# A gated attention-and-FFN block on one core: w2 turned by DMA, late scores on GpSimd, the last tile in halves

## The chip, the cores and the metric

The kernel runs on 1 core of one Trainium2 chip. The metric is the time of one execution on the device in microseconds, as the median of the runs.

## The reference

x is 4 x 512 rows of 512 values. First each row gets a term made of a sigmoid of pairwise scores and of its own normalised values; then a gated FFN with quantized weights (ternary) and quantized activations (8 bits) is added.

```python
def xattn(ctx, adj, W, b):                  # ctx: 4 x 512 x 128, adj = layernorm(x): 4 x 512 x 512
    si = einsum('bnd,d->bn', ctx, W[0, :128]);  sj = einsum('bnd,d->bn', ctx, W[0, 128:])
    return 0.6 * sigmoid(si[:, :, None] + sj[:, None, :] + b[0]) + 0.4 * adj
def weight_quant(w):
    scale = 1.0 / clip(mean(abs(w)), 1e-5);  return clip(round(w * scale), -1, 1) / scale
def bitlinear(x, w):                        # w1, w2: 1408 x 512, w3: 512 x 1408
    xn = x * rsqrt(mean(x * x, -1) + 1e-6);  s = 127 / clip(max(abs(xn), -1), 1e-5)
    return einsum('bsd,hd->bsh', clip(round(xn * s), -128, 127) / s, weight_quant(w))
x = x + tanh(g_xattn[0]) * xattn(ctx_512, layernorm(x), W, b)
y = layernorm(x)
x = x + tanh(g_ffn[0]) * bitlinear(silu(bitlinear(y, w1)) * bitlinear(y, w2), w3)
```

## The kernel before

The 2048 rows make 16 tiles of 128 rows, four to a batch. Tile i holds rows 128 i to 128 i + 127, one row to a partition. Everything runs from one program with an order written out by hand for each engine (SP from L322, GpSimd from L541, ScalarE from L763, VectorE from L1078, TensorE from L1354); semaphores tie them together. An engine that waits holds everything behind it in its order.

**Weights.** Each weight is loaded in four pieces (L295). The absolute values are summed by ScalarE (L643) and VectorE (L967), a matmul with ones adds over partitions (L1243), and VectorE makes the scale (`scale_w`, L975). w1 is turned by TensorE from float32, one row block of 128 at a time (`turn_rows`, L1265), and quantized on the way out of PSUM (L658, L1006) with a clip behind it (L1012). w2 is quantized in place, in six groups of two row blocks (`conv_w`, L505 and L992; GpSimd has groups 1 to 4), turned by TensorE (`turn_w`, L1276) and written out by ScalarE with a sign (L653) or by VectorE with a limit (L1001). w3 is quantized by GpSimd, clipped by VectorE (L1021) and turned by DMA (`turn_w3`, L302).

**Scores.** TensorE turns the context of a batch (`turn_ctx`, L1208), makes both scores as products (`scores`, L1218), and spreads them as a row over all partitions (`spread_scores`, L1228); ScalarE copies that row to SBUF (L685) and makes tanh of row plus own score for each tile (`score`, L689), in a ring of four.

**A tile.** `stats_x` (L918) and GpSimd's `slopes_x` (L435) give the layer norm's slope, `intercept` (L927) its offset; an affine and `make_x` (L945) give the new x, `max_x` (L957) and `square_x` its scale, `quant_x` (L488) the quantized tile, which SP turns by DMA (`turn_x`, L306). Tiles go in units (L41): 0; 1; 2 and 3; 4 and 5; and so on in pairs. TensorE makes the gate product into three banks and the up product into three others (`product`, L1294); ScalarE's `silu` (L716) empties the first, VectorE's `hidden` (L1028) the second, so gate product t + 1 waits for silu(t) and up product t + 1 for hidden(t). `max_h` (L1041), `quant_h` (L515) and `turn_h` (L312) prepare the last product (L1323), eleven matmuls of 512 columns; `finish` (L735) and `add_x` (L536, L1050) scale and add, and `store` (L318) writes the tile. The last tile's hidden values are turned by TensorE in two parts (`turn_last`, L1344).

GpSimd's `dequant_up(0)` (L473) is what `hidden(0)` waits for beside the up product, and `hidden_floors` (L429) writes two constants behind each slot of the ring `hid`, which lies where w2 was loaded, so it waits until w2 has been read.

## Time and profile before

| | |
|---|---|
| median of 3 runs | 158.2 us (157.78 to 158.7) |
| span of the profiled execution | 155.3 us |
| TensorE, VectorE busy | 139.7 us, 117.9 us |
| ScalarE, GpSimd busy | 107.3 us, 101.0 us |
| mean granted clock of TensorE | 0.978 |
| DMA | 26.94 MB, of it 13.89 MB read from HBM |

The profile is one execution; the difference of span and median lies before the first and behind the last instruction. In the rows, PE is TensorE, DVE VectorE, ACT ScalarE, POOL GpSimd, SPq the queue of SyncE, which issues the DMAs. L and a number is the line of the kernel. A granted clock of 1.00 is 2.4 GHz and of 0.50 is 1.2 GHz. Rows of a timeline that stand behind each other on an engine overlap by up to 0.1 us, so a step is read from start to start.

### The profile page before, as it was taken

How to read it: one execution, taken by the hardware profiler on the slowest of the kernel's cores; microseconds unless marked ns; L12 is line 12 of the kernel's file. 1: busy time of each engine (PE TensorE's matmuls, PEld its weight loads, DVE VectorE, ACT ScalarE, POOL GpSimd, SP SyncE). 2: the span in 40 equal slices, each digit the busy share in tenths (PEclk: the TensorE clock that was granted, in tenths of full speed). 3: DMA queues.
4: the chain of work that ended last, by engine and by line, in shares of the span. 5: the costliest groups of instructions: out<-in, count | busy, mean ns of one | idle time of the engine just before them, and what ended most of it. 6: DMA issues, size and time to landing. Idle time of an engine off the chain costs nothing.

```text
span 155.3 us, 2445 instructions
## 1 busy us (share of the span) xinstructions
PE 139.7 (90%) x743; PEld 76.7 (49%) x743; DVE 117.9 (76%) x180; ACT 107.3 (69%) x177; POOL 101.0 (65%) x155
## 2 busy tenths in 40 slices
PE   0984965798998999999999999999999999999991
PEld 0883854365555455444444444444454444454540
DVE  0338998998889999999979966489579184669441
ACT  3279998979598489967799286532999636772720
POOL 3302617999892791785989985669968999436210
PEclk9999599779999999999999999999999999999999
DMA  4899999999214189733193695453362807654313
GB/s 146 289 406 395 407 402 414 392 364 347 61 38 93 34 168 212 151 62 69 35 199 64 152 113 146 100 104 126 101 160 60 241 9 189 160 97 93 135 74 129
DMA packets 45237, 26.94 MB, mean 173 GB/s; under 512 B 35751, under 2 KB 37800, under 8 KB 45224
## 3 DMA queue, kind: packets, MB, share of 16 engines
q1 hardware_dynamic: 45216, 26.78, 60.9%
q8 instruction: 6, 0.10, 0.3%
q14 instruction: 7, 0.06, 0.1%
q10 hardware_dynamic: 8, 0.00, 0.0%
HBM read 13.89 MB, written 4.19 MB: 116 GB/s over the span
## 4 chain that ended last, share of the span: by engine, by line
PE 72%; DVE 11%; DMA 5%; POOL 4%; issue 3%; ACT 2%; SPq 1%; DVEq 0%; ACTq 0%; POOLq 0%
PE ps L1307 46%; PE ps L1341 24%; DMA raw_room<-in_L_ffn_w_dram 5%; DVE raw L1038 2%; DVE bn L922 2%; ACT w2T L656 1%; DVE w_abs L972 1%; POOL ln_r L440 1%; DVE w3q L1026 1%; DVE c_all L953 1%; DVE w1T L1009 1%; POOL raw L509 1%; DVE x_top L962 1%; PE ps L1290 1%; POOL slope L443 1%
## 5 line engine op out<-in xcount | busy, mean ns | idle before, releaser
L1307 PE MATMUL ps<-w1T,xqT 128*128 128x512 f16 (+1 forms) x192 | 42.3, 372 | 0.0
L1307 PE MATMUL ps<-w2T,xqT 128*128 128x512 f16 (+1 forms) x192 | 40.7, 361 | 1.1 <-ACT w2T L656 0.6
L1341 PE MATMUL ps<-w3T,hqT 128*128 128x512 f16 x176 | 40.1, 379 | 0.0
L1038 DVE SCALAR_TENSOR_TENSOR raw<-ps,deq,raw_room 128x1408 f32<-128x1408 f32 x16 | 26.9, 1683 | 16.6 <-PE ps L1307 11.2
L721 ACT ACTIVATE raw_room<-ps,deq 128x1408 f32<-128x1408 f32 x16 | 22.9, 1432 | 15.9 <-PE ps L1307 15.8
L521 POOL TENSOR_SCALAR hq<-raw,h_scale 128x1408 f16<-128x1408 f32 x15 | 23.8, 1590 | 9.9 <-DVE h_scale L1048 9.6
L1307 PEld LDWEIGHTS ps<-w1T,xqT 128*128 128x128 f16 x192 | 19.2, 100 | 20.6 <-issue 2.2
L1307 PEld LDWEIGHTS ps<-w2T,xqT 128*128 128x128 f16 x192 | 18.6, 98 | 20.9 <-DVE raw L1038 0.8
L1341 PEld LDWEIGHTS ps<-w3T,hqT 128*128 128x128 f16 x176 | 17.2, 98 | 19.3
L1045 DVE TENSOR_REDUCE h_top<-raw 128x1 f32<-128x1409 f32 x16 | 25.8, 1610 | 0.2
L732 ACT ACTIVATE junk<-raw 128x1410 f16<-128x1410 f32 x16 | 21.9, 1372 | 1.5 <-DVE raw L1038 1.3
L741 ACT ACTIVATE out_ring<-ps,x_mean,h_deq 128x512 f32<-128x512 f32 x14 | 10.8, 773 | 13.4 <-DMA out_dram<-out_ring 8.1
L494 POOL TENSOR_SCALAR xq<-c_all,x_scale 128x512 f16<-128x512 f32 x16 | 11.1, 695 | 10.9 <-DVE x_scale L965 10.6
L922 DVE BATCH_NORM_STATS2 bn<-c_all 128x6 f32<-128x512 f32 x16 | 10.3, 678 | 4.2 <-DMA c_all<-in_x_dram 4.2
L539 POOL TENSOR_TENSOR out_ring<-out_ring,c_all 128x512 f32<-128x512 f32 x9 | 12.4, 1375 | 0.0
L953 DVE SCALAR_TENSOR_TENSOR c_all<-th_ring,t,c_all 128x1024 f32<-128x1024 f32 (+1 forms) x9 | 10.4, 1158 | 0.6 <-ACT c_all L682 0.5
L455 POOL TENSOR_SCALAR c_all<-c_all,slope,icept 128x512 f32<-128x512 f32 x8 | 6.3, 796 | 6.2 <-DVE icept L935 6.2
L708 ACT ACTIVATE junk_x<-c_all 128x514 f16<-128x514 f32 x16 | 10.0, 622 | 0.6 <-DVE c_all L953 0.6
L962 DVE TENSOR_REDUCE x_top<-c_all 128x2 f32<-128x1026 f32 (+1 forms) x9 | 9.8, 1091 | 0.1
L532 POOL TENSOR_TENSOR h_r<-h_sq,minus_half 128x2 f32<-128x2 f32 (+1 forms) x9 | 6.1, 678 | 5.7 <-ACT junk L732 5.7
L651 ACT ACTIVATE junk<-raw 128x1408 f16<-128x1408 f32 (+2 forms) x6 | 8.2, 1358 | 1.4 <-DMA raw<-in_L_ffn_w_dram 1.3
L699 ACT ACTIVATE th_ring<-sj_wide,s_half 128x512 f32<-128x512 f32 x12 | 8.6, 716 | 0.7 <-DVE c_all L953 0.7
(99 smaller groups left out, 173.5 us busy)
## 6 DMA issues: line engine op xcount, KB each, us to landing
c_all<-in_x_dram SPq DMA_DIRECT2D x16, 256.0 KB, 9.5
out_dram<-out_ring SPq DMA_DIRECT2D x16, 256.0 KB, 2.1
raw<-in_L_ffn_w_dram SPq DMA_DIRECT2D x4, 704.0 KB, 11.2
raw_room<-in_L_ffn_w_dram SPq DMA_DIRECT2D x3, 768.0 KB, 8.2
raw<-in_L_ffn_w_dram SPq DMA_DIRECT2D x3, 768.0 KB, 11.7
hq<-in_ctx_dram SPq DMA_DIRECT2D x4, 256.0 KB, 10.2
raw_room<-in_L_ffn_w_dram SPq DMA_DIRECT2D x1, 512.0 KB, 10.3
raw<-in_L_ffn_w_dram SPq DMA_DIRECT2D x1, 512.0 KB, 10.6
```

What stands on the lines that cost most here:

```text
L494: g.tensor_scalar(xq[:, i % XQ, :], c_all[:, i, 0:D], x_scale[:, i:i + 1], QMAX * TINY, ALU.mult, ALU.mult).then_inc(xq_done, 1)
L521: g.tensor_scalar(hq[:, t % HQ, :], hid[:, t % HS, 0:H], h_scale[:, t:t + 1], QMAX * TINY, ALU.mult, ALU.mult).then_inc(hq_done, 1)
L539: g.tensor_tensor(o, o, c_all[:, t, 0:D], ALU.add).then_inc(out_done[t % OUTS], 1)
L721: s.activation(gate[:, t % GATES, :], ps_gate[:, 0:H], ACT.Silu, scale=deq[:, 0, t:t + 1]).then_inc(silu_done, 1)
L732: s.activation(junk[:, t % 2, 0:H + 2], hid[:, t % HS, 0:H + 2], ACT.Square, scale=H_SQUARE, accum_out=h_sq[:, t:t + 1]).then_inc(h_sq_don ...
L922: v.bn_stats(bn[:, i, :], c_all[:, i, 0:D]).then_inc(bn_done, 1)
L953: v.scalar_tensor_tensor(out=c_all[:, lo:hi, 0:D], in0=th_ring[:, lo % 4:lo % 4 + hi - lo, :], scalar=t03[:, 0:1], in1=c_all[:, lo:hi, 0:D ...
L962: v.tensor_reduce(out=x_top[:, lo:hi], in_=c_all[:, lo:hi, 0:D + 1], axis=AX_X, op=ALU.max, apply_absolute_value=True).then_inc(x_topped, 1)
L1038: v.scalar_tensor_tensor(out=hid[:, t % HS, 0:H], in0=ps_up[:, 0:H], scalar=deq[:, 1, t:t + 1], in1=gate[:, t % GATES, :], op0=ALU.mult, o ...
L1045: v.tensor_reduce(out=h_top[:, t:t + 1], in_=hid[:, t % HS, 0:H + 1], axis=AX_X, op=ALU.max, apply_absolute_value=True).then_inc(h_topped, 1)
L1307: last = m.matmul(bank[:, lo:hi], xqT[:, i % XT, k, :], wT[w][:, k, lo:hi], start=(k == 0), stop=(k == KD - 1))
L1341: last = m.matmul(ps_y[t % 2], hqT[:, t % HT, k, :], w3T[:, :, k, :], start=(k == 0), stop=(k == KH - 1))
```

## The change

- **Rows four to a partition.** A tile holds every fourth row of a batch, so a partition holds four neighbouring rows over the four tiles. The pieces of x and of the output stay 2 KB; a context load has one piece of 2 KB in a partition and not four of 512 B. ScalarE therefore reads spread scores from PSUM with a stride.
- **w2.** Quantized into a tile of its own, w2q (in the place of hqT), by VectorE (groups 0 and 5), ScalarE (1) and GpSimd (2 to 4); VectorE clips each group (`clip_w2`); SP turns it by DMA in three chunks of 4, 4 and 3 row blocks (`turn_w2`). TensorE no longer turns it, and nobody writes it out of PSUM. The three parts of up product 0 wait for one chunk each. `hidden_floors` waits for all six clips.
- **Late scores.** For batches 2 and 3 GpSimd multiplies the context by W (`ctx_product`), VectorE sums (`sum_scores`), SP stores the row of scores to DRAM (`store_sj`) and loads it back to all partitions (`spread_sj`).
- **The last tile.** Quantized by VectorE in one instruction, turned by DMA; its product is made in two halves of 256 columns in two banks, and `finish` and `store` work by halves (`finish_half`, `store_half`).
- **Loads.** Tiles 4 and 5 come before w3; W, the context of batch 2 and tiles 6 and 7 behind it, and the turns of w2 stand before tiles 8 to 15. The context of batch 3 comes much later.
- All five engines have new orders.

```diff
--- before.py
+++ after.py
...
-    x_t = x.rearrange("b (t p) d -> (b t) p d", p=P)
-    out_t = out.rearrange("b (t p) d -> (b t) p d", p=P)
-    ctx_t = ctx_in.rearrange("b (t p) d -> b p t d", p=P)
+    x_rows = x.rearrange("b (p t) d -> b t p d", p=P)
+    out_rows = out.rearrange("b (p t) d -> b t p d", p=P)
+    x_t = [x_rows[i // TB, i % TB] for i in range(T)]
+    out_t = [out_rows[i // TB, i % TB] for i in range(T)]
+    ctx_t = ctx_in.rearrange("b (p t) d -> b p t d", p=P)
+    sj_rows = nc.dram_tensor("sj_rows", (B, N), F32, kind="Internal").ap()
...
-    CONV_POOL = [[], [1, 2, 3, 4], [0, 1, 2, 3]]
+    CONV_ACT = [[], [1], []]
+    CONV_POOL = [[], [2, 3, 4], [0, 1, 2, 3]]
...
+    PRODUCTS = 2
+    LATE = [n for n in range(B) if n >= PRODUCTS]
+    HALF = D // 2
+    TURNS = [(0, 2), (2, 4), (4, 6)]
...
-        w2T = sb("w2T", [P, KD, H], F16)
+        w2T = sb("w2T", [P, KH, KD, P], F16)
...
+        w2q = hqT[:, :, :, :].rearrange("p s k c -> p (s k c)").rearrange("p (t d) -> p t d", d=D)
...
+        w_wide = sb("w_wide", [P, 2, DC])
+        ctx_w = hqT[:, 2:4, :, :].rearrange("p s k c -> p (s k c)")[:, 0:4 * TB * DC].bitcast(F32).rearrange(
+            "p (u t d) -> p u t d", t=TB, u=2)
+        s_sums = sb("s_sums", [P, B, 2, TB])
...
+            def store_sj(n):
+
+                sp.wait_ge(scores_sb, n + 1)
+                sp.dma_start(sj_rows[n].rearrange("(p t) -> p t", p=P),
+                             s_half[:, n, 1, :]).then_inc(sj_stored[n - PRODUCTS], 16)
+
+            def spread_sj(n):
+
+                sp.wait_ge(sj_stored[n - PRODUCTS], 16)
+                sp.dma_start(sj_wide[:, n - len(DIRECT), :],
+                             sj_rows[n:n + 1].broadcast_to([P, N])).then_inc(sj_in[n - PRODUCTS], 16)
+
+            def turn_w2(c):
+
+                sp.wait_ge(w2_clip, TURNS[c][1])
+                lo, hi = CHUNKS[c][0] // P, CHUNKS[c][1] // P
+                sp.dma_start_transpose(w2T[:, lo:hi, :, :].rearrange("p t k c -> p (t k) c"),
+                                       w2q[:, lo:hi, :].rearrange("p t d -> p (t d)")).then_inc(w2_in[c], 16)
...
             def turn_h(t):
-                sp.wait_ge(hq_done, t + 1)
+                if t == T - 1:
+                    sp.wait_ge(hq_last, 1)
+                else:
+                    sp.wait_ge(hq_done, t + 1)
+                if t == 0:
+                    for c in range(len(CHUNKS)):
+                        sp.wait_ge(w2_in[c], 16)
+                if t == 2:
+                    sp.wait_ge(s_summed, len(LATE))
...
             def hidden_floors():
 
-                pool.wait_ge(wT_ps, NG)
+                pool.wait_ge(w2_clip, NG)
...
-                    g.tensor_scalar(raw_low[w][:, lo:hi, :], raw[w][:, lo:hi, :], w_scale[:, w:w + 1], 1.0, ALU.mult,
-                                    ALU.mult).then_inc(w_q_pool, 1)
+                    g.tensor_scalar(w2q[:, lo:hi, :], raw[w][:, lo:hi, :], w_scale[:, w:w + 1], TINY, ALU.mult,
+                                    ALU.min).then_inc(w_q_pool, 1)
...
+            def ctx_product(n):
+
+                if n == PRODUCTS:
+                    pool.wait_ge(w_wide_in, 16)
+                    for c in range(len(CHUNKS)):
+                        pool.wait_ge(w2_in[c], 16)
+                else:
+                    pool.wait_ge(s_summed, n - PRODUCTS)
+                pool.wait_ge(ctx_ld[n], 16)
+                g.tensor_tensor(ctx_w[:, :, :, :], ctx_sb[n].rearrange("p (u t) d -> p u t d", u=1).broadcast_to([P, 2, TB, DC]),
+                                w_wide[:, :, :].rearrange("p u (t d) -> p u t d", t=1).broadcast_to([P, 2, TB, DC]),
+                                ALU.mult).then_inc(ctx_times_w, 1)
...
+            def conv_w(w, n):
+                act.wait_ge(w_scaled, w + 1)
+                lo, hi = GROUPS[n]
+                s.activation(w2q[:, lo:hi, :], raw[w][:, lo:hi, :], ACT.Copy, scale=w_scale[:, w:w + 1]).then_inc(w_q_act, 1)
...
+                if n in DIRECT:
+                    act.wait_ge(sj_ps, n + 1)
+                    s.activation(th_ring[:, i % 4, :].rearrange("p (c k) -> p c k", k=TB),
+                                 ps_y[1].rearrange("p (k c) -> p c k", k=TB), ACT.Tanh, bias=s_half[:, n, 0, i % TB:i % TB + 1],
...
+            def sum_scores(n):
+
+                dve.wait_ge(ctx_times_w, n - PRODUCTS + 1)
+                v.tensor_reduce(out=s_sums[:, n, :, :], in_=ctx_w[:, :, :, :], axis=AX_X, op=ALU.add).then_inc(s_summed, 1)
+                dve.wait_ge(s_summed, n - PRODUCTS + 1)
+                v.tensor_scalar(s_half[:, n, :, :], s_sums[:, n, :, :], 0.5, b_quarter[:, 0:1], ALU.mult, ALU.add).then_inc(scores_sb, 1)
...
+            def clip_w2(n):
+                lo, hi = GROUPS[n]
+                if n in CONV_DVE[1]:
+                    dve.wait_ge(w_q_dve, count(CONV_DVE, 1, n))
+                elif n in CONV_ACT[1]:
+                    dve.wait_ge(w_q_act, count(CONV_ACT, 1, n))
+                else:
+                    dve.wait_ge(w_q_pool, count(CONV_POOL, 1, n))
+                v.tensor_scalar(w2q[:, lo:hi, :], w2q[:, lo:hi, :], TINY, -TINY, ALU.min, ALU.max).then_inc(w2_clip, 1)
...
-                            w_left(w, NG - 1)
+                            rows_left([9, 10, 5][c])
+                            pe.wait_ge(w2_in[c], 16)
...
-                if t < T - 1:
-                    pe.wait_ge(hT_in[t % HQ], 16 * (t // HQ + 1))
+                pe.wait_ge(hT_in[t % HQ], 16 * (t // HQ + 1))
+                if t == T - 1:
+                    pe.wait_ge(silu_done, T)
+                    for n in range(2):
+                        for k in range(KH):
+                            last = m.matmul(ps_last[n], hqT[:, t % HT, k, :],
+                                            w3T[:, n * KD // 2:(n + 1) * KD // 2, k, :], start=(k == 0), stop=(k == KH - 1))
+                        last.then_inc(y_ps, 1)
+                    return
...
```

Of the new orders, the stretches that the prediction speaks of. Numbers are the arguments; x, h and w are the tiles, a pair (w, n) a weight and its part.

```
SP:     w3 (4 loads), load_w_wide, load_ctx 2, load_x 6 7, turn_w2 0 1 2, load_x 8 9, turn_x 2, load_x 10 11, turn_x 3,
        turn_w3 0, load_x 12, turn_w3 1, turn_x 4, load_x 13 14, turn_w3 2, turn_x 5, load_x 15, store_sj 2, turn_h 0,
        turn_w3 3, load_ctx 3, turn_x 6, spread_sj 2, turn_h 1, turn_x 7, turn_h 2, store_sj 3, spread_sj 3, turn_h 3,
        turn_h 4, turn_x 8, store 0, turn_h 5, ... turn_h 14, store 9, turn_h 15, store 10 to 14, store_half 0 1
GpSimd: ... quant_x 1, conv_w (1,2), slopes_x 2, conv_w (1,3) (1,4), hidden_floors, affine_x 2 3, dequant_gate 0, step_x 1,
        slopes_x 3, conv_w (2,0), dequant_x 1, dequant_up 0, quant_x 2, conv_w (2,1), step_x 2, quant_x 3, dequant_x 2,
        conv_w (2,2), ctx_product 2, step_x 3, quant_x 4 5, dequant_x 3, quant_h 0, conv_w (2,3), dequant_h 0, step_x 4,
        quant_x 6, quant_h 1 2, mean_x 0, ctx_product 3, slopes_x 4, dequant_x 4, quant_h 3, quant_x 7, affine_x 8 9, ...
VectorE: ... scale_w 1, stats_x 2, weight_factor 0, conv_w (1,0), clip_w2 0, evac_rows 10, clip_w1 2, conv_w (1,5),
        clip_w2 1, sum_w (2,0), intercept 2, clip_w2 2 3, weight_factor 1, clip_w2 4 5, stats_x 3 4, make_x 2, scale_w 2,
        weight_factor 2, max_x 2, intercept 3, hidden 0, clip_w3 0 1, make_x 3, intercept 4, hidden 1, max_h 0, max_x 3,
        hidden 2, max_h 1, sum_scores 2, clip_w3 2, hidden 3, make_x 4, clip_w3 3, max_x 4, hidden 4, max_h 2 3,
        stats_x 5 6, hidden 5, sum_scores 3, intercept 5, max_h 4, intercept 6, make_x 5, hidden 6, max_h 5, max_x 5, ...
ScalarE: ... evac_x 0, evac_rows 8, sum_w (2,0), scores_out 1, evac_rows 9, conv_w (1,1), th_neg_x 0, square_x 1,
        sum_w (2,1), evac_x 1, sum_w (2,2), silu 0, score 4 5 6, square_x 2, affine_x 4, score 7, affine_x 5, silu 1, ...
        silu 15, finish 11 12, square_h 14 15, finish 13
TensorE: ... turn_rows 10, gate 0, turn_x 1, sum_w 2, up 0, gate 1, up 1, ... gate 5, up 5, last 0, gate 6, last 1, up 6,
        gate 7, last 2, up 7, last 3, gate 8, last 4, up 8, ... gate 11, up 11, last 5, last 6, gate 12, last 7, up 12, ...
        last 10, gate 15, up 15, last 11 to 15
```

## Rows read from the trace of the kernel before

**Rows 1.** The page, part 1: busy us, share of the span, instructions of each engine.

```profile
PE 139.7 (90%) x743; PEld 76.7 (49%) x743; DVE 117.9 (76%) x180; ACT 107.3 (69%) x177; POOL 101.0 (65%) x155
```

**Rows 2.** The table of windows, one stretch: busy us of each engine, clock, DMA, GB/s.

```profile
48.49:151.95 103.46, 103.44 (x515) 49.85 (x515) 80.22 (x102) 69.39 (x109) 72.04 (x99) 1.00 0.53 119
```

**Rows 3.** The chain of waits in order of time: start us, us, what.

```profile
60.55 0.44 PE ps L1232 x4
...
125.19 14.26 PE ps L1307 x72
...
146.57 0.61 PE ps L1350 x11
147.19 4.76 PE ps L1341 x22
...
152.07 0.75 DVE out_ring L1075
```

**Rows 4.** The timeline of PE, the first gate and up product: start us, us, what.

```profile
28.91 4.23 PE L1307 MATMUL ps<-w1T,xqT 128*128 128x512 f16 x12
...
36.72 2.54 PE L1307 MATMUL ps<-w2T,xqT 128*128 128x512 f16 x12 [0.61 <-ACT w2T L656]
```

**Rows 5.** The table of windows inside the first gate product.

```profile
30.00:31.00 1.00, 1.00 (x4) 0.34 (x3) 1.00 (x1) 1.00 (x3) 1.00 (x2) 0.50 1.06 369
```

**Rows 6.** The timeline of DVE, w2's scale and the steps of a tile.

```profile
24.98 0.16 DVE L982 RECIPROCAL w_scale<-w_step 128x1 f32<-128x1 f32 x1
...
69.45 1.68 DVE L1038 SCALAR_TENSOR_TENSOR raw<-ps,deq,raw_room 128x1408 f32<-128x1408 f32 x1
71.05 0.45 DVE L935 TENSOR_SCALAR icept<-th_sum,t_neg,slope_mean 128x1 f32<-128x1 f32 x2
71.42 1.61 DVE L1045 TENSOR_REDUCE h_top<-raw 128x1 f32<-128x1409 f32 x1
...
73.17 1.28 DVE L953 SCALAR_TENSOR_TENSOR c_all<-th_ring,t,c_all 128x1024 f32<-128x1024 f32 x1
74.37 1.28 DVE L922 BATCH_NORM_STATS2 bn<-c_all 128x6 f32<-128x512 f32 x2
...
75.78 1.19 DVE L962 TENSOR_REDUCE x_top<-c_all 128x2 f32<-128x1026 f32 x1
...
77.09 1.60 DVE L1045 TENSOR_REDUCE h_top<-raw 128x1 f32<-128x1409 f32 x1
```

**Rows 7.** Line L1026: duration ns min/median/max, first and last start.

```profile
L1026 DVE TENSOR_SCALAR w3q<-w3q x4: 506/1078/1315, 45.1 to 57.5; 128x1408 f16<-128x1408 f16 x4
```

**Rows 8.** The timeline of POOL: conversions, quantizations, and the first and last of slopes.

```profile
26.91 6.33 POOL L509 TENSOR_SCALAR raw<-raw,w_scale 128x1024 f16<-128x1024 f32 x4
...
65.44 0.70 POOL L494 TENSOR_SCALAR xq<-c_all,x_scale 128x512 f16<-128x512 f32 x1
66.11 1.44 POOL L521 TENSOR_SCALAR hq<-raw,h_scale 128x1408 f16<-128x1408 f32 x1
...
67.79 0.25 POOL L439 TENSOR_SCALAR ln_ve<-ln 128x4 f32<-128x4 f32 x1 [0.24 <-DVE ln L925]
...
69.62 0.20 POOL L444 TENSOR_TENSOR slope_mean<-slope,ln 128x4 f32<-128x4 f32 x1
```

**Rows 9.** Line L539: duration ns min/median/max, first and last start.

```profile
L539 POOL TENSOR_TENSOR out_ring<-out_ring,c_all x9: 1262/1274/2181, 77.1 to 131.1; 128x512 f32<-128x512 f32 x9
```

**Rows 10.** The DMA issues by line: what, count, KB, median us to landing.

```profile
hqT<-hq SPq DMA_TRANSPOSE x15, 3.5
xqT<-xq SPq DMA_TRANSPOSE x14, 2.4
...
out_dram<-out_ring SPq DMA_DIRECT2D x16, 256.0 KB, 2.1
```

**Rows 11.** The table of windows while hqT, w3T and xqT are turned together.

```profile
60.00:62.00 2.00, 2.00 (x14) 1.25 (x12) 1.89 (x4) 2.00 (x4) 0.44 (x1) 1.00 1.13 214
```

**Rows 12.** The groups by line: the spread scores read by ACT from PSUM.

```profile
L699 ACT ACTIVATE th_ring<-ps,s_half 128x512 f32<-128x512 f32 x4 | 2.7, 673 | 0.0
```

626 lines of the change are left out of this document (286 added, 340 removed).

## The prediction

> **What bounds the kernel now.** I read the page first: TensorE is busy 139.7 of 155.3 us, VectorE 117.9 [rows 1]. The table of windows then says where TensorE has room: from 48.49 to 151.95 us it is busy 103.44 of 103.46 us at a granted clock of 1.00 [rows 2]. The chain of waits agrees: from there it is TensorE's, with no wait on another engine, until the last `finish` [rows 3]. A product (12 matmuls, or 11 against w3) steps 2.375 us there (six in 14.26 [rows 3]), so 43 products take 102.1 us, and two insertions stand between them: spreading the scores of batch 3 (0.44) and turning the last tile (0.61) [rows 3]. So the end is set by (a) when the unbroken stretch begins and (b) what stands in it besides products. Before it, VectorE, ScalarE, GpSimd and the loads take turns: the first gate product starts at 28.91 and takes 4.2 us [rows 4] because the granted clock is 0.50 (1.2 GHz) in it [rows 5], and the first up product starts at 36.72.
>
> The span is 155.3; the median of the runs is 158.2, so 2.9 us lie outside. I add a change of the span to 158.2. A measurement of this kernel can tell about 0.5% (0.8 us) from no change.
>
> **TensorE's own savings.** Gone from it: 44 transposes of w2, the context transposes, score products and spreads of batches 2 and 3, and the 11 transposes of the last tile. Those before 48.49 us count only if the new start of the unbroken stretch is set by TensorE; I find below that it isn't. In the stretch 0.44 + 0.61 = 1.05 us go. The last product as 22 matmuls of 256 columns moves the same columns: 0. The up products read w2T in pieces of 128 columns now, as the products with w3T do, and those step 2.38 [rows 3]: 0. The last `finish` covers 256 columns, about 0.45 instead of 0.75 us [rows 3]: 0.3 us less.
>
> **When the stretch begins.** I lay the new orders out engine by engine, with steps from start to start in the rows. Up to the scale of w2 little changes: VectorE has it at 25.1 us now [rows 6] and at 25.5 in the new order. Then w2 takes the new way. VectorE: statistics of tiles 2 and 3 to 27.0, conversion and clip of group 0 to 28.1, row block 10 to 28.7. ScalarE reaches row block 9 only at about 29.4, since it first sums the first w3 piece, and the w3 loads come 0.26 MB later, about 0.7 us at 369 GB/s [rows 5]; w1's last clip then ends at 29.9, conversion of group 5 and clip of group 1 at 31.5, the sum of w3's piece at 33.0, an intercept at 33.4, and clips of groups 2 to 5 at 34.9 (0.35 each, 0.51 of [rows 7] cut to 1024 elements). GpSimd's three conversions at 1.4 to 1.6 us [rows 8] end by about 32.
>
> Clips have a range: the four of w3 took 0.51 to 1.32 us for 1408 elements [rows 7]; the six new ones have 1024 or 512. At 0.35 GpSimd stands idle beside the last four; the upper end is 0.9 more for each of the six, 3 us in all if none found it idle. The long ones of w3 ran beside GpSimd's conversions and quantizations. The Trainium skill, "SBUF — State Buffer", section "SBUF: two separate sides", says that a VectorE instruction of this kind and one of GpSimd exclude each other for their whole length; the trace agrees, 0.51 against 1.32. By that rule the last four clips, with GpSimd waiting, stay short.
>
> The DMA turns three chunks of 16, 16 and 12 blocks. A turn of 11 blocks lands 3.5 us after its issue, one of 4 blocks 2.4 [rows 10], and back to back they move 214 GB/s with all 16 engines taken [rows 11]. The last chunk, issued at about 35.5 behind two of 2.5 us each, lands at 39.5 (bounds 38.4, issue plus 3.5, and 41). So the first up product ends at 40.0, against 39.1 now.
>
> Behind the clips comes the dearer part. GpSimd's `hidden_floors` waits for all six clips, with all its work queued behind it: two affines (36.8), the gate factor (37.1), step_x 37.9, the slopes of four tiles (2.0 by [rows 8], 39.95), w3's first conversion (41.4), the up factor (41.9). `hidden(0)` waits for that last one: 41.9 to 43.5. The second gate product runs 40.0 to 42.4, or 44.1 if the clock is at 1.2 GHz as in the first [rows 4, 5], since TensorE has only the chunks of one product between 31 and 40 us. Up product 1 starts at 43.5 to 44.1 and ends 46.2; gate product 2 ends 48.6 (`silu(1)` 45.2 and the turn of tile 2 at 45.0 are in time); `hidden(1)` ends 47.8. So up product 2 starts at **48.6** against 48.49: +0.1. Both the lost clock and most of the saved PE work vanish here. If w2 or GpSimd are 1.5 us quicker or later, this start moves by that.
>
> The Trainium skill, "TensorE: Matmul & The Clock Gate", section "What's actually happening", says that an idle engine falls to 1.2 GHz. The trace agrees that the level falls behind thin work [rows 5].
>
> **Inside the stretch.** TensorE wants, from 48.6 in steps of 2.375: g4 at 55.7, u4 58.1, u5 62.9, L0 65.2, L1 70.0, u6 72.4, g7 74.7, L2, u7, L3, g8 at 84.2 (g gate, u up, L last products). The engines behind it, by [rows 6, 8]: VectorE does `hidden` in 1.60, `max_h` 1.75, `make_x` 1.20, two `stats` 1.41, `max_x` 1.31 (pairs of tiles). The two sums of scores are new: a reduce of 1024 elements and a small one, 1.4 us each, and `ctx_product` (1024 outputs from two inputs) has no like in the trace; the nearest row is GpSimd's addition of two 512-wide tiles, 1.27 [rows 9], so 2.5 for its 1024 outputs, bounds 2.0 (the two fixed starts counted once) and 4.4 (one such addition took 2.18).
> - GpSimd ends w3's third conversion at 49.4, `ctx_product(2)` at 51.9, step_x 52.7, `quant_x(4)` 53.4; turned by 55.8: g4 waits 0.1.
> - VectorE from there: hidden(2) 52.6, max_h(1) 54.3, scores 55.7, clip 56.4, hidden(3) 58.0, make_x 59.2, clip 59.8, max_x 61.1, hidden(4) 62.7 (just in time for u5), max_h(2) 64.4, max_h(3) 66.1, stats of units 5 and 6 at 68.9, hidden(5) 70.5.
> - GpSimd: `quant_h(2)` 65.9, `ctx_product(3)` 68.6, then `slopes_x(4)`, which needs those stats: 70.95; factors 71.15; `quant_h(3)` 72.6; `quant_x(7)` 73.3 (1.44 and 0.70 by [rows 8]); the turn of tile 7 lands at 75.7. g7 wants to start at 74.7: **1.0 us of stall**. Now `quant_x(7)` is done at 66.1 [rows 8], long before its product.
> - SP: `turn_h(2)` (its slot holds ctx_w) waits for the second sum of scores, 71.9, and stands behind turn_x(7): lands 78.2, L2 wants 78.1. Behind it `spread_sj(3)` waits for its store (2.1 us, as an output store [rows 10]), with turn_h(3) (L3) and turn_x(8) (g8) queued: lands 82.9 and 84.5, wanted at 82.8 and 85.2. No cost, no slack.
> - After g8 VectorE is ahead again (hidden(7) 89.5, wanted 90.5).
> - The end: last tile turned by DMA: hidden(15) 1.6, max_h 1.75, quantization 0.9, turn 3.5 [rows 10] = 7.8 us, behind four products (9.5): hidden. `finish(13)` now follows both last squares on ScalarE and a store; 0.2 us in hand, price up to 1.
>
> The other moves cost nothing that I can see. Strided rows of x keep pieces of 2 KB, and those of ctx grow from 512 B to 2 KB; the context's gain of some 0.1 us ends in front of w1's loads. ScalarE now reads the spread scores from PSUM with a stride, five times, 0.6 to 0.7 us each now [rows 12]: bounds 0 and 0.7 more for each, 3 us in all, of which two reads (1.4) precede w1's sum; no row has such a read, I take 0 as the count of elements is the same.
>
> **Sum**: +0.1 (start) - 1.05 (insertions) + 0.1 + 1.0 (g4, g7) - 0.3 (tail) = -0.15 us. Span 155.15, time 158.05, which I round to **158.0**.
>
> **Rivals.**
> 1. *The covers hold* (faster). Up product 2 starts 1 to 2 us sooner (the last turn lands at 38.4, clock stays high) and the stall of g7 is not there because VectorE's chain starts sooner too: -0.15 - 1.0 - 1.5 = -2.65, 155.5. For it: GpSimd and ScalarE are only 65% and 69% busy [rows 1]. Against: three serial waits in front of `hidden(0)`. Range 154.5 to 157.3. Chance 0.31.
> 2. *GpSimd's products are dear* (slower). At 4.4 instead of 2.5 us, quant_x(4) is 1.9 late for g4 and quant_x(7) again for g7 (its slopes then start at 70.5): +1.9 + 1.5 = 3.4, 161.5. It decides from 3.0 us a product on. For it: one addition of 2.18 us; against: the median of nine is 1.27 [rows 9], and its place beside VectorE's one-input reduces. With queue stalls at L2 and L3 of 1 us: 159 to 161. Chance 0.25.
> 3. *The queue of SP is the bound*: turn_h(2) to turn_x(8) late by more than the 0.1 of slack, 0.5 to 2 us, 158.6 to 160. It decides from a `sum_scores(3)` 0.5 us late. Chance 0.06 beside what lies in 2, 0.02 of it still within the bound.
> 4. *The change of w2 is no different way*: the turn hides wholly and the start is as now, no stall: -1.35, 156.85; in 1.
>
> My own case has 0.38 (156.9 to 159.0), 0.06 of it below 157.4, where faster begins. So faster 0.31 + 0.06, same 0.32 + 0.02, slower 0.25 + 0.04. Range for 8 in 10: 154.8 to 161.0; my likeliest case alone 156.9 to 159.0.
>
> **What would show it.** The first up product ending at about 40 with gaps between its three chunks; GpSimd idle some 3 us before `hidden_floors`; `hidden(0)` released by GpSimd; up product 2 at 48 to 49.5; TensorE's idle just before gate product 7 released by a DMA of xqT; two GpSimd products of 2.5 us; the last PE insertion gone. Wrong if TensorE is unbroken from before 47 us, if the products take over 3 us, or if L2 or L3 wait on hqT by over 0.5.

## The result, and the profile after

The changed kernel takes **167.1 us** (median of 4 runs, 166.68 to 167.44) against 158.45 of the kernel before on the same chip (157.78 to 160.47): ratio 1.0593, interval 1.0539 to 1.0646. It is slower by 6%; forecast were 158.0 us and a range that ended at 161.0. Ratios leave out executions more than 1.5% above the fastest of their kernel, and medians count them, which matters for e7, e11 and e15 below (159.06, 160.9 and 161.7 us without them).

The profiled execution took 166.95 us, its span 165.1, so 1.85 us lie outside the span. The 2.9 us that the prediction took for the kernel before are a median less the span of one execution: in the 62 executions of the kernel before that ran beside the experiments 1.7 to 1.9 us lie outside. So its profiled execution, with a span of 155.3, must have been one of the quick ones, at about 157.1 us, an estimate; the spans differ by 9.8 us and the medians by 8.65.

The page, part 1 and the row of TensorE's clock in part 2 (the kernel before: [rows 1]):

```profile
PE 138.3 (84%) x667; PEld 72.3 (44%) x667; DVE 121.2 (73%) x184; ACT 102.0 (62%) x170; POOL 109.3 (66%) x156
...
PEclk9998775985589999999999999999999999999999
```

TensorE's instructions fell from 743 to 667, as the diff says. GpSimd's busy time rose by 8.3 us, though its two new products of the context with W take only 4.7. The clock is low twice, in slices 5 to 7, which end at 28.9 us, and again in slices 10 and 11, 37 to 45 us, where up product 0 runs.

The timeline of TensorE: start us, us, what, and in brackets the idle time before it and what ended it. It answers [rows 4] and, for the end, [rows 3]:

```profile
36.89 1.86 PE L1354 MATMUL ps<-w2T,xqT 128*128 128x512 f16 x4 [2.14 <-DMA w2T<-hqT]
41.28 1.87 PE L1354 MATMUL ps<-w2T,xqT 128*128 128x512 f16 x4 [2.53 <-DMA w2T<-hqT]
43.69 1.44 PE L1354 MATMUL ps<-w2T,xqT 128*128 128x384 f16 x4 [0.54 <-DMA w2T<-hqT]
44.92 3.23 PE L1354 MATMUL ps<-w1T,xqT 128*128 128x512 f16 x12
49.33 2.55 PE L1354 MATMUL ps<-w2T,xqT 128*128 128x512 f16 x12 [1.19 <-DVE raw L1105]
...
54.09 2.54 PE L1354 MATMUL ps<-w2T,xqT 128*128 128x512 f16 x12
...
64.46 2.55 PE L1354 MATMUL ps<-w2T,xqT 128*128 128x512 f16 x12 [0.70 <-DVE raw L1105]
...
72.78 2.53 PE L1389 MATMUL ps<-w3T,hqT 128*128 128x512 f16 x11 [0.90 <-DMA w3T<-w3q]
...
83.19 2.54 PE L1354 MATMUL ps<-w1T,xqT 128*128 128x512 f16 x12 [0.75 <-DMA xqT<-xq]
...
91.28 2.53 PE L1389 MATMUL ps<-w3T,hqT 128*128 128x512 f16 x11 [0.67 <-DMA hqT<-hq]
...
101.44 2.54 PE L1354 MATMUL ps<-w1T,xqT 128*128 128x512 f16 x12 [0.50 <-DMA xqT<-xq]
...
159.62 2.58 PE L1384 MATMUL ps<-w3T,hqT 128*128 128x256 f16 x22 [1.00 <-ACT out_ring L812]
```

The reader is to see three things. Up product 0 comes in three pieces and ends at 45.1, not 40.0. Up product 2 starts at 54.09, not 48.6; the kernel before has 48.49 [rows 2]. And behind it stand six waits where the kernel before has none. In the names below, gate, up and last product t are the three products of tile t.

I measure each kernel below by two numbers. The **start** is the start of up product 2. The **loss** is what TensorE takes from there to its last matmul, beyond 102.4 us; that is 103.44 of [rows 2] less the 1.05 of the two insertions that the change takes out. The kernel before has a start of 48.49 and would have a loss of 0. The changed kernel, with its last matmul ending at 162.20, has a start of 54.09 and a loss of 5.7. The whole difference of the spans is then 5.6 (start) + 5.7 (loss) - 1.05 (insertions) - 0.5 (tail: 2.9 instead of 3.4 us behind the last matmul) = 9.8 us.

Where the start went is in GpSimd's timeline, to be held against [rows 8]:

```profile
26.02 3.73 POOL L560 TENSOR_SCALAR hqT<-raw,w_scale 128x1024 f16<-128x1024 f32 x1
...
31.76 7.40 POOL L560 TENSOR_SCALAR hqT<-raw,w_scale 128x1024 f16<-128x1024 f32 x2
39.88 0.11 POOL L483 MEMSET raw<- 128x4 f32 x1 [0.72 <-DVE hqT L1071]
...
40.00 1.52 POOL L506 TENSOR_SCALAR c_all<-c_all,slope,icept 128x512 f32<-128x512 f32 x2
...
47.25 0.31 POOL L528 TENSOR_SCALAR deq<-x_step,w_deq 128x1 f32<-128x1 f32 x1
```

A conversion of w2 takes 3.72 us, not the 1.4 to 1.6 that I read off [rows 8]. Everything behind it is as forecast but five us late: `hidden_floors` at 39.88 (forecast 34.9), the up factor at 47.25 (41.9), `hidden(0)` released by it at 47.59. Up product 0 had ended at 45.1, before that, so in the changed kernel the chain through GpSimd alone sets the start.

### The profile page after: what moved, and what is told of

Read it like the earlier page. It is cut to its first block, busy times and chain, and to the rows that moved or that the text cites. A ratio compares the mean times of both kernels' runs of the same rounds, so it can differ in the third digit from the quotient of the medians.

```text
span 165.1 us, 2297 instructions
## 1 busy us (share of the span) xinstructions
PE 138.3 (84%) x667; PEld 72.3 (44%) x667; DVE 121.2 (73%) x184; ACT 102.0 (62%) x170; POOL 109.3 (66%) x156
## 4 chain that ended last, share of the span: by engine, by line
PE 32%; DVE 17%; POOL 16%; DMA 16%; SPq 8%; issue 5%; ACT 3%; ACTq 0%; DVEq 0%; POOLq 0%
PE ps L1354 20%; PE ps L1389 9%; POOL hqT L560 7%; DMA raw_room<-in_L_ffn_w_dram 6%; DVE raw L1105 4%; DVE h_top L1112 3%; SPq L351 3%; DMA sj_wide<-sj_rows 2%; POOL ln_r L491 2%; DMA raw<-in_ctx_dram 2%; DMA out_dram<-out_ring 2%; SPq L331 2%; DVE w1T L1076 2%; SPq L337 2%; PE ps L1384 2%
## 5 line engine op out<-in xcount | busy, mean ns | idle before, releaser
L1354 PE MATMUL ps<-w2T,xqT 128*128 128x512 f16 (+1 forms) x192 | 43.3, 375 | 7.1 <-DMA w2T<-hqT 5.2
L1354 PE MATMUL ps<-w1T,xqT 128*128 128x512 f16 (+1 forms) x192 | 42.6, 372 | 1.6 <-DMA xqT<-xq 1.3
L1389 PE MATMUL ps<-w3T,hqT 128*128 128x512 f16 x165 | 37.4, 379 | 1.6 <-DMA w3T<-w3q 0.9
L585 POOL TENSOR_SCALAR hq<-raw,h_scale 128x1408 f16<-128x1408 f32 x15 | 21.6, 1442 | 11.8 <-DVE h_scale L1115 11.6
L1389 PEld LDWEIGHTS ps<-w3T,hqT 128*128 128x128 f16 x165 | 15.9, 98 | 20.5 <-issue 2.6
L545 POOL TENSOR_SCALAR xq<-c_all,x_scale 128x512 f16<-128x512 f32 x16 | 11.8, 737 | 2.8 <-DVE x_scale L1027 2.2
L515 POOL TENSOR_TENSOR rnorm<-x_sq,minus_half 128x2 f32<-128x2 f32 (+1 forms) x9 | 7.1, 784 | 9.5 <-ACT junk_x L777 8.2
L1015 DVE SCALAR_TENSOR_TENSOR c_all<-th_ring,t,c_all 128x1024 f32<-128x1024 f32 (+1 forms) x9 | 11.5, 1276 | 1.3 <-POOL c_all L506 1.2
L603 POOL TENSOR_TENSOR out_ring<-out_ring,c_all 128x512 f32<-128x512 f32 x9 | 11.4, 1271 | 0.0
L560 POOL TENSOR_SCALAR hqT<-raw,w_scale 128x1024 f16<-128x1024 f32 x3 | 11.1, 3720 | 0.1
L596 POOL TENSOR_TENSOR h_r<-h_sq,minus_half 128x2 f32<-128x2 f32 (+1 forms) x9 | 7.1, 787 | 4.6 <-ACT junk L801 4.4
```

Of the source, the lines that this page charges most:

```text
L545: g.tensor_scalar(xq[:, i % XQ, :], c_all[:, i, 0:D], x_scale[:, i:i + 1], QMAX * TINY, ALU.mult, ALU.mult).then_inc(xq_done, 1)
L560: g.tensor_scalar(w2q[:, lo:hi, :], raw[w][:, lo:hi, :], w_scale[:, w:w + 1], TINY, ALU.mult, ALU.min).then_inc(w_q_pool, 1)
L585: g.tensor_scalar(hq[:, t % HQ, :], hid[:, t % HS, 0:H], h_scale[:, t:t + 1], QMAX * TINY, ALU.mult, ALU.mult).then_inc(hq_done, 1)
L603: g.tensor_tensor(o, o, c_all[:, t, 0:D], ALU.add).then_inc(out_done[t % OUTS], 1)
L1015: v.scalar_tensor_tensor(out=c_all[:, lo:hi, 0:D], in0=th_ring[:, lo % 4:lo % 4 + hi - lo, :], scalar=t03[:, 0:1], in1=c_all[:, lo:hi, 0:D ...
L1354: last = m.matmul(bank[:, lo:hi], xqT[:, i % XT, k, :], side, start=(k == 0), stop=(k == KD - 1))
```

## The experiments

The runs stand on five chips, each time with the kernel before beside them: e1 to e4; e5 to e8; e9 to e12; e13 to e15; e16 to e18. The kernel before had medians of 157.6 to 158.2 us there, so kernels of different groups are compared by their ratios to it. Start and loss come from one profiled execution of each kernel.

### The instruction: e1_mult, e2_max, e3_before_min

The conversion was changed in one more way than the place of its result: its second operation, a multiplication by 1.0, became a minimum with TINY. e1 puts the multiplication back into the changed kernel; the clip behind it limits both sides anyway.

```diff
-  g.tensor_scalar(w2q[:, lo:hi, :], raw[w][:, lo:hi, :], w_scale[:, w:w + 1], TINY, ALU.mult, ALU.min)
+  g.tensor_scalar(w2q[:, lo:hi, :], raw[w][:, lo:hi, :], w_scale[:, w:w + 1], 1.0, ALU.mult, ALU.mult)
```

> The changed kernel with one edit: GpSimd's conversion of w2 multiplies by 1.0 behind the scale and doesn't take the minimum with TINY (VectorE's clip behind it does that anyway, so the result is the same). Theory A: the second operation min is what makes that instruction 3.72 us; then it takes 1.4 us, the last clip ends near 34.5 and not 39.8, up product 2 starts at 48.5 to 49.5 and not 54.1, and the span falls by about 5 us to 160. Rival B: the place is the cause (output packed into hqT, or VectorE beside it): then the conversions stay at 3.7 us and the span at 165.

e2 has the changed kernel with `-TINY, ALU.mult, ALU.max`; e3 has the kernel before with `TINY, ALU.mult, ALU.min` in L509 and nothing else.

> As the changed kernel, but GpSimd's second operation is max with -TINY and not min with TINY; the result is the same, since VectorE's clip takes both. If every comparison costs what min does, 3.7 us for 1024 elements and a span near 165; if only min does, 1.4 us and a span near 160. Rival B expects 3.7 us here too, so this run is read beside the one with the multiplication.

> The kernel before with one edit: its four GpSimd conversions of w2, whose output is strided and stays in place, take min with TINY as second operation. The sign behind them makes the result the same. Theory A: 3.7 us each and not 1.4, 9 us more on GpSimd before the affines of tiles 2 and 3; TensorE's unbroken stretch starts 7 to 9 us later than 48.5, and the ratio to the kernel before is 1.045 to 1.06. Rival B (packed output or the neighbour): 1.4 us as now, ratio 1.00.

The line of the conversion in each (duration ns min/median/max, first and last start), e1, e2, e3:

```profile
L560 POOL TENSOR_SCALAR hqT<-raw,w_scale x3: 1117/1276/1355, 26.1 to 31.3; 128x1024 f16<-128x1024 f32 x3
```

```profile
L560 POOL TENSOR_SCALAR hqT<-raw,w_scale x3: 3698/3715/3737, 26.1 to 35.5; 128x1024 f16<-128x1024 f32 x3
```

```profile
L509 POOL TENSOR_SCALAR raw<-raw,w_scale x4: 3979/3988/4015, 26.7 to 38.5; 128x1024 f16<-128x1024 f32 x4
```

Measured: e1 165.03 us, ratio to the kernel before 1.0459 (1.0417 to 1.0502); e2 166.62 in a single execution; e3 168.45, 1.0675 (1.0623 to 1.0728). The multiplication takes 1.1 to 1.4 us, minimum and maximum 3.7, and the minimum takes as long in the kernel before, where the result has a stride and the place is another. So it is the operation and neither the place nor the stride. Alone it makes the kernel before slower by 6.75%: its up product 2 starts at 59.60, 11.1 us later for four conversions that take 9.6 us more together, where I had expected 7 to 9.

But in the changed kernel the multiplication gives back only 2.1 us of 8.7. In e1 the last clip ends at 34.6 and the up factor at 42.1, both as forecast (34.9 and 41.9), and yet up product 2 starts at 51.15 (expected were 48.5 to 49.5) and the loss is 6.5. The floors come 5.1 us earlier than in the changed kernel (34.77 for 39.88), but the start only 2.9, and 0.8 of those are lost again inside the stretch. e1's up product 0 says where: it begins at 36.86, waits 2.27 us for w2's later chunks and ends at 44.1, at 1.2 GHz.

### Two orders: e4_orders

Two waits had been named: gate product 7, whose quantization stands behind `ctx_product(3)` and `slopes_x(4)`, and the last product, whose bank is held by `finish(13)`, which waits for `store(10)`, which SP issues behind `turn_h(15)`. e4 is e1 with:

```diff
@@ GpSimd
             quant_x(6)
+            quant_x(7)
             quant_h(1)
@@ SP
+            store(10)
             turn_h(15)
-            store(10)
```

> The kernel with the multiplication and two moves: GpSimd quantizes tile 7 right behind tile 6 and not behind the second context product, and SP issues store 10 before the turn of the last tile and not behind it. Theory: the stall before gate product 7 (0.9 us in the changed kernel) and that before last product 15 (1.2 us, finish 13 waiting for store 10) were set by these two places, so both go and the span is 1.5 to 2.1 us under that of the kernel with the multiplication alone. Rival: other engines are as late, the stalls move to the next product, and less than 0.7 us is gained.

Measured: 161.21 us, 1.0243 (1.0192 to 1.0295). Both waits are gone, and the loss is 2.8. The profiled execution was the fastest of its six (159.88) and began at 49.92; most kernels with the same start section began at 51.2 to 52.3 (e9, e12, e15, e17 below). Against e1 the median fell by 3.8 us and the profiled span by 4.9: 1.2 in the start and 3.7 in the loss. The two waits account for 1.7 of the 3.7 (0.60 and 1.14 from start to start in e1; 0.91 and 1.16 in the changed kernel). The wait for tile 5's turn also shrank, from 1.71 to 0.23 us, and no edit touched it. So the two orders are worth about 2 us, and the rest is variation from execution to execution, in the start and in that wait. Why the start varies is the next question.

### The start: e5_turns_first, e6_filler, e7_no_turn_wait

In e4 up product 0 begins at 38.29, 3.33 us after TensorE was free, and then runs at 1.2 GHz. Three things could be meant by "w2's turn is late": DMA traffic in front of it, the clock, or the wait itself.

e5 issues the three turns ahead of the loads of W, context 2 and tiles 6 and 7:

```diff
             load_w(2, 3)
+            turn_w2(0)
+            turn_w2(1)
+            turn_w2(2)
             load_w_wide()
             load_ctx(2)
             load_x(6)
             load_x(7)
-            turn_w2(0)
-            turn_w2(1)
-            turn_w2(2)
```

> e4_orders with one more change on SP: the three turns of w2 are issued ahead of the loads of W's two rows, of context 2 and of row tiles 6 and 7 (0.83 MB) instead of behind them. In e4_orders the first turn was issued at 30.91 and its product began at 38.29, and the three issues took 1.5, 3.1 and 3.7 us. Theory A: the turns stand behind the bulk loads in the same DMA engines; 0.83 MB at about 400 GB/s is 2.1 us, so product 0 up begins at 36.2 to 36.9 and the stretch 1 to 2 us earlier: ratio to e4_orders 0.988 to 0.994. Rival B: a turn of a half-precision weight with other traffic takes its 5 us whatever stands ahead of it: product 0 up begins within 0.5 us of 38.3 and the time is that of e4_orders (161.2).

Measured: 170.27 us, 1.0778 (1.0735 to 1.0821), worse than anything else. Both theories missed. Up product 0 did begin 3 us earlier (35.30), but SP now stood in the turns until 37.1, and VectorE's timeline shows who needed the loads behind them:

```profile
33.70 1.27 DVE L984 BATCH_NORM_STATS2 bn<-c_all 128x6 f32<-128x512 f32 x2
...
43.83 0.69 DVE L984 BATCH_NORM_STATS2 bn<-c_all 128x6 f32<-128x512 f32 x1 [8.64 <-DMA c_all<-in_x_dram]
```

The statistics of tiles 6 and 7 stand ahead of `hidden(0)` in VectorE's order; it waited 8.64 us for them. I had asked only when the tiles' products need them. What the run does show is that up product 0 ends only at 42.6 even when the three turns are issued without those loads ahead.

e6 puts 25 matmuls that nobody reads (filler) on TensorE, in its idle time ahead of up product 0:

```diff
             turn_x(1, "sums", 2)
+            rows_left(5)
+            filler(13)
             sum_w(2, "x", 2)
+            filler(12)
             up_product(0)
```

with `filler(n)` n matmuls of 128x512 into the last bank of `ps_up`, which product 0 overwrites.

> e4_orders with 25 products of 128x512 that nobody reads, put on TensorE ahead of product 0 up (13 behind the turn of row tile 1, 12 behind w3's sum), where TensorE stood idle from 31.3 to 38.3. They add work and take no wait away. Theory A: what TensorE loses at the start is not only the wait on w2's turns but its clock, which was 0.50 in 36:40 and 0.68 in 40:44, after the idle time; with it kept up product 0 up takes 2.5 instead of 4.66 us and ends by 41; hidden(0) is then bound by dequant_up(0) at 41.8, and product 1 up begins at about 43.6 instead of 45.16: 158.8 to 160 us. Rival B: the clock stays low here whatever TensorE does, and the time is that of e4_orders or, where the products get in the way, up to 1 us more.

The windows of e4 and of e6, the same stretch (us, busy us of each engine, clock, DMA, GB/s):

```profile
36.00:44.00 8.00, 5.71 (x18) 1.98 (x19) 5.29 (x14) 6.38 (x13) 7.37 (x12) 0.59 1.02 187
```

```profile
36.00:44.00 8.00, 5.89 (x28) 2.33 (x26) 6.40 (x17) 6.39 (x13) 7.37 (x13) 1.00 1.01 180
```

And TensorE's timeline in e6:

```profile
38.55 1.02 PE L1354 MATMUL ps<-w2T,xqT 128*128 128x512 f16 x4 [0.80 <-DMA w2T<-hqT]
40.24 1.02 PE L1354 MATMUL ps<-w2T,xqT 128*128 128x512 f16 x4 [0.66 <-DMA w2T<-hqT]
41.91 0.81 PE L1354 MATMUL ps<-w2T,xqT 128*128 128x384 f16 x4 [0.65 <-DMA w2T<-hqT]
```

Measured: 159.66 us, 1.0089 (1.0057 to 1.0121), with work added. By the ratios that is 1.5% or 2.4 us below e4; the plain difference of the medians, 1.55 us, is taken across two chips. The clock is 1.00 and each piece of up product 0 runs at 2.4 GHz as soon as its chunk is there: 38.5, 40.2, 41.9. So the three chunks land 1.7 us apart, the last at **41.9, where I had forecast 39.5**. From there to up product 2 at 49.69 TensorE has no wait, so in e6 that landing sets the start. Against e4's profiled execution the clock gives nearly nothing (its stretch begins at 49.92, e6's at 49.69). What the clock gives is against e4's other executions: without filler, up product 0 often begins earlier (36.6 to 37), waits again in the middle, and it and gate product 1 run at 1.2 GHz; it ends at 43.9 to 44.4 (e1, e9, e12, e15, e17) instead of 42.4 to 42.7 with filler (e6, e10, e18).

e7 makes up product 0 from w1's turned weight, so that it waits for no turn; tile 0's output is another:

```diff
-                            pe.wait_ge(w2_in[c], 16)
@@
-    side = w1T[:, k, lo:hi] if w == 0 else w2T[:, lo // P:hi // P, k, :]
+    side = w1T[:, k, lo:hi] if w == 0 or i == 0 else w2T[:, lo // P:hi // P, k, :]
```

> e4_orders with product 0 up computed from w1's turned weight instead of w2's, so that it waits for none of w2's turns; product 1 up waits for all three. Row tile 0's output is then another. It prices the wait that the DMA turn put in the place of TensorE's own turns. Theory A: product 0 up begins at about 35 to 36, product 1 gate follows silu(0) at 37.5, and the next limit is dequant_up(0) at 41.8 and hidden(0) behind it: product 1 up begins at 43.6 to 44 instead of 45.16, so the wait is worth 1.2 to 1.6 us as the rest stands, not its 3.3 us of idle time. Rival B: hidden(0) is not held by anything else, and the gain is 3 us or more.

Measured: 159.44 us, 1.0091 (1.0056 to 1.0127), by the ratios the same 1.5% below e4 as e6. Up product 1 begins at 44.28 after waiting 2.99 us for `hidden(0)`: the next limit, `dequant_up(0)`, stands right behind the turns, as theory A had it; and behind that wait up product 1 runs mostly at 1.2 GHz (4.24 us). Taking away the whole wait is worth no more than keeping the clock.

### The orders in the stretch: e8, e9, e10

e8 is e4 with `ctx_product(2)` moved into an idle 3.4 us of GpSimd ahead of `step_x(2)`, `quant_x(9)` behind `quant_x(8)`, `turn_w3(3)` ahead of `store_sj(2)`, `turn_h(3)` ahead of `spread_sj(3)`:

```diff
@@ GpSimd
             conv_w(2, 1)
+            ctx_product(2)
             step_x(2)
@@
             conv_w(2, 2)
-            ctx_product(2)
             step_x(3)
```

> e4_orders with four steps put elsewhere: on GpSimd ctx_product(2) ahead of step_x(2), where the engine stood idle for 3.42 us, and quant_x(9) right behind quant_x(8); on SP turn_w3(3) ahead of store_sj(2) and turn_h(0), and turn_h(3) ahead of spread_sj(3). In e4_orders TensorE waited 0.61 us for row tile 4's turn, 0.23, 0.51 for w3's last turn and 0.75 for row tile 9's. Theory A: these are waits of the orders alone, each with its queue: they go, 1.5 to 2.1 us together, 159.1 to 159.8 us. Rival B: the engines behind (ScalarE's squares, the turn's 4 us) are late themselves, at most half of it comes back: 160.2 us or more.

Measured: 161.41 us, 1.0213 (1.0166 to 1.0259): no clear gain on e4 (1.0243), loss 3.9 instead of 2.8. The timeline of VectorE and GpSimd in e8:

```profile
44.41 3.21 DVE L1093 TENSOR_SCALAR w3q<-w3q 128x1408 f16<-128x1408 f16 x2
...
44.60 2.63 POOL L575 TENSOR_TENSOR hqT<-out_ring,w_wide 128x1024 f32<-128x1024 f32 x1
```

and the same two clips in e4, where no product of GpSimd ran beside them:

```profile
44.69 0.95 DVE L1093 TENSOR_SCALAR w3q<-w3q 128x1408 f16<-128x1408 f16 x2
```

Two half-precision clips take 0.95 us alone and 3.21 beside the product; they end 0.4 us after it. The idle time of GpSimd was no free place. The Trainium skill, "SBUF — State Buffer", section "SBUF: two separate sides", says that the two engines lock each other out of a shared port for the length of such an instruction; the trace agrees, 0.95 against 3.21, and the product, issued behind the first clip, takes 2.63 instead of 2.36 us. The forecast had used the rule for the clips of w2 only.

e9 keeps e8's three other moves and puts `ctx_product(2)` behind `quant_h(0)`, to keep it from the clips; e10 is e9 with e6's filler:

```diff
@@ GpSimd
             conv_w(2, 2)
-            ctx_product(2)
+            conv_w(2, 3)
             step_x(3)
...
             quant_h(0)
-            conv_w(2, 3)
+            ctx_product(2)
@@ VectorE
-            sum_scores(2)
             clip_w3(2)
+            clip_w3(3)
             hidden(3)
             make_x(4)
-            clip_w3(3)
+            sum_scores(2)
```

> e4_orders with five steps put elsewhere, chosen so that no product of GpSimd runs beside VectorE's clips of w3: on GpSimd conv_w(2, 3) in the idle stretch ahead of step_x(3), ctx_product(2) behind quant_h(0), quant_x(9) right behind quant_x(8); on VectorE the clips of w3's last two pieces ahead of hidden(3) and sum_scores(2) behind make_x(4); on SP turn_w3(3) ahead of store_sj(2), turn_h(3) ahead of spread_sj(3). In e8_orders2 ctx_product(2) at 44.60:47.23 ran beside two clips of w3, which took 3.21 instead of 0.95 us, and everything on VectorE behind them was late; its waits were 3.9 us in the stretch where e4_orders had 2.1. Theory A: e8's orders failed by that collision alone; without it the waits for row tiles 4 and 9 and for w3's last turn go: 159.2 to 160.2 us, 1 to 2 us below e4_orders. Rival B: any order of these steps gives back as much elsewhere: 161 us or more.

> e9_orders3 with the 25 products nobody reads of e6_filler. e6_filler was 1.5 us below e4_orders, with the clock at 1.00 from 36 to 46. Theory A: the two gains are of different stretches and add: 157.6 to 158.8 us, which would be level with the kernel before (158.2). Rival B: what the clock gave was the earlier start of a chain that the new orders shorten too: 159 us or more.

Measured: e9 163.01 us, 1.0337 (1.0285 to 1.0390); e10 160.69, 1.0181 (1.0125 to 1.0237). The filler is worth 2.3 us here, but the orders lost again, and by the same collision, one stage later. VectorE and GpSimd in e10:

```profile
55.34 3.59 DVE L1093 TENSOR_SCALAR w3q<-w3q 128x1408 f16<-128x1408 f16 x2
...
55.93 2.63 POOL L575 TENSOR_TENSOR hqT<-out_ring,w_wide 128x1024 f32<-128x1024 f32 x1
```

I had timed both by e4's rows, and both had moved.

### One part undone, one part shortened: e11, e12

e11 is e4 with w2's clipped groups turned by TensorE and written out of PSUM by VectorE (0, 1, 5) and ScalarE (2, 3, 4). The core of the edit:

```diff
-            turn_w2(0)
-            turn_w2(1)
-            turn_w2(2)
@@ TensorE
+            def turn_w2(n):
+                pe.wait_ge(w2_clip, n + 1)
+                for t in range(lo, hi):
+                    for d in range(KD):
+                        last = m.transpose(bank[:, at:at + P], w2q[:, t, d * P:(d + 1) * P], ident16[:, :])
```

> e4_orders with one part of the change undone: w2's clipped half-precision weight is turned by TensorE (six groups of 8 or 4 transposes, in the time in which it stood idle) and moved from PSUM by VectorE (groups 0, 1, 5) and ScalarE (2, 3, 4), instead of by three DMA turns. Rows of before price the evacuations at 0.67, 0.67 and 0.41 us on VectorE and 1.02 us each on ScalarE. Theory A: w2 by DMA is what made the start late: its last piece landed at 41.9 to 42.5 where 39.5 was forecast. Turned by TensorE the last group is there by 37.5, product 0 up begins there at 2.4 GHz and ends at about 40.2, and the limit is dequant_up(0) at 41.8 with hidden(0) to 43.5: product 1 up begins at 43.5 to 44 instead of 45.16, 159 to 160 us. Rival B: the 3.1 us of evacuations on ScalarE push silu(0) from 36.1 to 37.5 and all its squares as far back, so that row tiles 3 to 5 are later instead: 160.5 us or more.

Measured: 161.38 us, 1.0196 (1.0127 to 1.0265), the same as e4. TensorE's timeline shows why an up product 0 that ends 3 us earlier brought nothing:

```profile
37.42 2.54 PE L1364 MATMUL ps<-w2T,xqT 128*128 128x512 f16 x12 [1.44 <-ACT w2T L713]
...
45.05 4.12 PE L1364 MATMUL ps<-w2T,xqT 128*128 128x512 f16 x12 [2.71 <-DVE raw L1112]
```

Up product 0 runs at 37.42, at 2.4 GHz, and ends at 39.9. Then up product 1 waits 2.71 us for `hidden(0)`, which began at 43.30, when `dequant_up(0)` was done; and after that idle time TensorE runs it mostly at 1.2 GHz (4.12 instead of 2.54 us, mean granted clock 0.59 from 45 to 49). Up product 2 then starts only at 51.38.

e12 is e4 with both `ctx_product`s cut to 16 outputs; the sums behind them stay whole:

```diff
-  g.tensor_tensor(ctx_w[:, :, :, :], ...broadcast_to([P, 2, TB, DC]), ...broadcast_to([P, 2, TB, DC]), ALU.mult)
+  g.tensor_tensor(ctx_w[:, 0, 0, 0:16], ctx_sb[n][:, 0, 0:16], w_wide[:, 0, 0:16], ALU.mult)
```

> e4_orders with ctx_product(2) and (3) cut from 1024 outputs each to 16, so that the scores of batches 2 and 3 are sums of other numbers: it leaves out GpSimd's multiplication for half of the scores and keeps every wait. It prices the products where they stand. Theory A: ctx_product(2), 2.36 us at 51.01, pushes quant_x(4) and so the wait of 0.61 us at 57.82; and the whole is worth 0.6 to 1.2 us: 160.0 to 160.6 us. Rival B: the products lie beside other work, and the time is that of e4_orders within 0.3 us. Rival C (the forecast's second rival): they are dear, and 2 us or more come back.

Measured: 162.44 us, 1.0313 (1.0257 to 1.0370), not below e4 at all; loss 3.1, with the same waits for tiles 4, 5 and 9 and for w3. By its number no expectation fits: by the ratios it is 1.1 us above e4, where rival B allowed 0.3. Its start, at 51.88, was one of the late ones; nothing in the edit explains that. By mechanism it is rival B: the multiplications by themselves cost nothing where the changed kernel has them. That also settles my second rival of the forecast.

### Start and stretch together: e13 to e18

e13 is e11 with one step of GpSimd moved:

```diff
             dequant_gate(0)
+            dequant_up(0)
             step_x(1)
             slopes_x(3)
             conv_w(2, 0)
             dequant_x(1)
-            dequant_up(0)
```

> e11_w2_by_pe with dequant_up(0) moved on GpSimd from behind conv_w(2, 0) to right behind dequant_gate(0). In e11 product 0 up ended at 39.9 and product 1 gate at 42.3, but hidden(0) began at 43.30, as soon as dequant_up(0) (42.97) was there, after VectorE had been idle for 1.33 us, and product 1 up at 45.05, at 1.2 GHz for 4.12 us. Theory A: with w2's turn out of the way, this order is what holds the start: hidden(0) follows intercept(3) at 42.0, product 1 up begins at 43.7 and, after 1.4 us of idle time in place of 2.7, mostly at 2.4 GHz: 2 to 3 us less than e11, 158.5 to 159.5 us. Rival B: VectorE and ScalarE behind it are late as well, and the later waits take it back: 160.5 us or more.

Measured: 161.32 us, 1.0216 (1.0168 to 1.0265). Up product 1 begins at 43.91 as expected (43.7), the start is 49.51 instead of 51.38, and the loss is 4.0 instead of 2.8: the ratio is e11's. Rival B.

In the four kernels in which TensorE turns w2 (e11, e13, e14, e16) something more lies outside the span: 2.0 to 2.9 us in 14 of their 24 executions, where every execution of the other kernels has 1.7 to 1.9. So part of what they miss against the DMA's versions doesn't stand in the timelines at all, and its cause is open.

e15 keeps e4's start and has, beside e8's three other moves:

```diff
@@ VectorE
             hidden(1)
+            max_x(3)
             max_h(0)
-            max_x(3)
@@ GpSimd
             conv_w(2, 2)
-            ctx_product(2)
-            step_x(3)
             quant_x(4)
             quant_x(5)
+            ctx_product(2)
+            step_x(3)
```

e14 has these and e13's start, with `hidden(0)`, `hidden(1)` and `silu(1)` each moved ahead of what stood before it. e17 is e4 with one step moved:

```diff
             quant_x(2)
+            quant_x(3)
             conv_w(2, 1)
             step_x(2)
-            quant_x(3)
```

> e4_orders (w2 by DMA) with only the stretch's orders of e14: VectorE max_x(3) ahead of max_h(0); GpSimd quant_x(4) and (5) ahead of ctx_product(2), quant_x(9) behind quant_x(8); SP turn_w3(3) ahead of store_sj(2), turn_h(3) ahead of spread_sj(3). ctx_product(2) stays clear of the clips of w3. Theory A: what made row tiles 4, 5 and 9 late is that VectorE's maximum over them stood behind max_h(0), with hidden(0) 3.7 us later than in the kernel before: the waits of 0.61, 0.23, 0.51 and 0.75 us go and the rest stays: 1.5 to 2.1 us below e4_orders, 159.1 to 159.8 us. Rival B: another engine's lateness takes their place, as in e8 and e9: 161 us or more.

> e13_w2_pe_up with the orders around the start and in the stretch mended too. Start: VectorE max_x(2) and hidden(0) ahead of scale_w(2), hidden(1) ahead of make_x(3), max_x(3) ahead of max_h(0); ScalarE silu(1) ahead of the affines of row tiles 4 and 5; GpSimd quant_x(2) and dequant_x(1) ahead of conv_w(2, 0). Stretch: GpSimd quant_x(4) and (5) ahead of ctx_product(2), quant_x(9) behind quant_x(8); SP turn_w3(3) ahead of store_sj(2), turn_h(3) ahead of spread_sj(3). Theory A: w2's turn by DMA and the orders are the whole distance to the kernel before, and the rest of the change (late scores by GpSimd, last tile in halves) is worth its 1.0 us and 0.5 us: product 1 up begins at 42.5 to 43, waits in the stretch come to under 1 us, 155.5 to 157.5 us, under the kernel before (158.2). Rival B: the other parts cost something that no run so far has shown: 158.5 us or more.

> e4_orders with one step moved: quant_x(3) on GpSimd from behind step_x(2) to right behind quant_x(2). Theory A: SP's queue is what makes row tiles 4 and 5 late: turn_x(3) is issued at about 44 to 46 instead of 49.4 to 51.7, the two turns of w3 go in the time behind it, turn_x(4) and (5) follow their quantisations at once, and the waits for them (0.61 and 0.23 us, 1.96 in e15) shrink; 0.5 to 1.2 us below e4_orders, 160.0 to 160.7 us. Rival B: the quantisations themselves are late, behind VectorE's maximum, and nothing changes: 161.2 within 0.4 us.

Measured: e15 162.72 us, 1.0255 (1.0193 to 1.0318); e14 162.97, 1.0324 (1.0282 to 1.0366); e17 161.75, 1.0267 (1.0197 to 1.0336). None gained. In e14 up product 1 began at 42.93, the earliest of all, and then gate product 3 waited 3.16 us for `silu(2)`: I had moved `hidden(1)` ahead of `make_x(3)` and `intercept(4)`, and ScalarE stood 3.46 us at an affine that needs that offset, with `silu(2)` behind. In e17 SP did issue the turn of tile 3 at 45.03 instead of 49.37, so theory A's mechanism was real; the wait for tile 4 went, and one of 0.63 us for `hidden(3)` took its place.

e16 (w2 turned by TensorE) and e18 (by DMA, with filler) have all of these orders mended; against e14, `silu(2)` ahead of the affines of tiles 6 and 7, `quant_x(3)` behind `quant_x(2)`, `clip_w3(1)` behind `intercept(4)`, and `hidden(2)` ahead of `max_h(0)`.

> e13_w2_pe_up (w2 turned by TensorE, dequant_up(0) early) with every order mended that the traces named: quant_x(3) behind quant_x(2), dequant_x(1) ahead of it; silu(1) ahead of the affines of row tiles 4 and 5 and silu(2) ahead of those of 6 and 7; on VectorE max_x(2) and hidden(0) ahead of scale_w(2), hidden(1) ahead of make_x(3), max_x(3) and hidden(2) ahead of max_h(0); and the stretch's orders of e15. Theory A: product 1 up begins at 42.9 as in e14, product 2 up at 47.7 to 48.5 where the kernel before has 48.49, the waits behind it stay under 1 us, and with the 1.05 us of TensorE work that the change took out of the stretch it is at 155.5 to 157.5 us: level with the kernel before or under it. Rival B: the other parts of the change cost something no run has shown: 159 us or more.

> The same orders as e16_w2_pe_all with w2 turned by DMA as in the changed kernel, and the 25 products nobody reads of e6_filler ahead of product 0 up. Theory A: w2's last turn lands at 41.9 whatever the orders, product 0 up ends at 42.5, product 1 up begins at 44.9 and product 2 up at 49.7; against e16 it is 1.2 to 2 us more, 157.5 to 159 us. Rival B: the cover behind the start takes the difference up, and it is as fast as e16 within 0.5 us.

Measured: e16 160.40 us, 1.0185 (1.0120 to 1.0249), which is rival B; e18 161.44, 1.0216 (1.0160 to 1.0272), 1.0 us above e16, which neither theory had. e18 has the filler and the DMA's turns like e6 and starts at 49.71 like it (49.69), but its loss is 4.6 and not 3.1: all the mended orders together make e18 1.3% slower than e6, which has e4's. e16's profiled execution took 161.65, above its median, and has one large wait. TensorE, VectorE and GpSimd around it:

```profile
48.87 2.54 PE L1364 MATMUL ps<-w2T,xqT 128*128 128x512 f16 x12
...
61.30 4.12 PE L1364 MATMUL ps<-w2T,xqT 128*128 128x512 f16 x12 [2.76 <-DVE raw L1112]
...
56.59 1.20 DVE L976 TENSOR_REDUCE s_sums<-hqT 128x8 f32<-128x1024 f32 x1
57.83 1.41 DVE L978 TENSOR_SCALAR s_half<-s_sums,b_quarter 128x8 f32<-128x8 f32 x1
59.14 0.51 DVE L1100 TENSOR_SCALAR w3q<-w3q 128x1408 f16<-128x1408 f16 x1
59.57 1.67 DVE L1112 SCALAR_TENSOR_TENSOR raw<-ps,deq,raw_room 128x1408 f32<-128x1408 f32 x1
...
57.77 1.44 POOL L554 TENSOR_SCALAR w3q<-raw,w_scale 128x1408 f16<-128x1408 f32 x1
```

Up product 2 starts at 48.87, 0.38 us behind the kernel before, and up product 4 waits 2.76 us for `hidden(3)`. Ahead of `hidden(3)` VectorE does two `max_h` and then `sum_scores(2)`, which takes 2.6 us, since its second instruction, on 8 columns, takes 1.41 us beside GpSimd's conversion (0.23 in e4, where it begins ahead of the conversion). VectorE is busy 14.56 of the 15.03 us from 46.21 to 61.24. The wait and the slow product behind it (4.12 instead of 2.54) are 4.3 of e16's loss of 5.6.

## What the runs say together

| kernel | start | loss | start + loss | ratio to before |
|---|---|---|---|---|
| before | 48.49 | 1.05 (its insertions) | 49.5 | 1 |
| after | 54.09 | 5.7 | 59.8 | 1.0593 |
| e3 (before, minimum) | 59.60 | 1.06 (its insertions) | 60.7 | 1.0675 |
| e1 | 51.15 | 6.5 | 57.7 | 1.0459 |
| e4 | 49.92 | 2.8 | 52.7 | 1.0243 |
| e6 (filler) | 49.69 | 3.1 | 52.8 | 1.0089 |
| e7 (leaves out a wait) | 50.73 | 3.0 | 53.7 | 1.0091 |
| e11 (w2 by TensorE) | 51.38 | 2.8 | 54.2 | 1.0196 |
| e12 (short products) | 51.88 | 3.1 | 55.0 | 1.0313 |
| e17 | 51.59 | 3.2 | 54.8 | 1.0267 |
| e5 (turns first) | 60.51 | 3.2 | 63.7 | 1.0778 |
| e13 | 49.51 | 4.0 | 53.5 | 1.0216 |
| e15 | 52.29 | 3.8 | 56.1 | 1.0255 |
| e8 | 50.82 | 3.9 | 54.7 | 1.0213 |
| e9 | 51.21 | 4.7 | 55.9 | 1.0337 |
| e10 (e9 with filler) | 49.34 | 4.4 | 53.7 | 1.0181 |
| e18 (filler) | 49.71 | 4.6 | 54.3 | 1.0216 |
| e14 | 48.73 | 7.6 | 56.3 | 1.0324 |
| e16 | 48.87 | 5.6 | 54.5 | 1.0185 |

Three edits explain most of the 5.9%, each measured as a step: the multiplication in the conversion 1.3% (e1), two orders 2.2% (e4, of which their own waits explain 1.3%), filler that keeps the clock 1.5% (e6). 0.9% are left. No run undid the layout of the rows, the order of the loads or the last tile's halves by themselves, so what those cost or save isn't shown.

The six kernels with e4's orders in the stretch (e4, e6, e7, e11, e12, e17) start between 49.69 and 51.88 and lose 2.8 to 3.2 whatever their start, whoever turns w2; so does e5, which starts at 60.51. Every kernel whose orders I changed further loses 3.8 or more, and the two with the earliest starts, e14 and e16, lose most: each has one large wait, for `silu(2)` and for `hidden(3)`. I read this as something other than TensorE holding the first third, and the table of windows has a candidate: in the kernel before VectorE is busy 37.5 of the 40 us from 24 to 64. The rows of before, by tens (us, busy us of PE, PEld, DVE, ACT, POOL, clock, DMA, GB/s):

```profile
24.00:34.00 10.00, 7.65 (x60) 4.93 (x61) 9.45 (x19) 8.47 (x15) 9.03 (x10) 0.83 1.04 391
34.00:44.00 10.00, 9.36 (x62) 5.54 (x61) 9.03 (x20) 8.40 (x14) 9.24 (x16) 1.00 0.62 209
44.00:54.00 10.00, 9.55 (x55) 5.48 (x54) 9.37 (x15) 7.16 (x16) 5.74 (x12) 1.00 0.25 49
54.00:64.00 10.00, 10.00 (x54) 5.08 (x53) 9.65 (x10) 9.43 (x16) 6.24 (x7) 1.00 0.98 187
```

and of after:

```profile
34.00:44.00 10.00, 4.40 (x12) 1.34 (x13) 6.17 (x15) 2.46 (x6) 9.01 (x11) 0.60 0.78 152
```

VectorE had little slack up to 64 us, and the change makes it wait in 34 to 44. `hidden(3)` begins at 55.93 in the kernel before, 57.73 in e4, 59.57 in e16, 62.73 after; from 24 us to there VectorE is busy for 29.6, 30.0, 33.4 and 32.2 us. So in e4 its work up to `hidden(3)` is the same as before, in spite of the six clips, and it comes 1.8 us late because VectorE waited longer; in e16 VectorE has 3.4 us more ahead of `hidden(3)` than in e4: writing w2 out of PSUM (1.8), the slow instruction of `sum_scores(2)` (1.2) and slower clips. That a full VectorE is the bound of the stretch's first part is argued from these rows; no run took work from VectorE alone, so it isn't shown. No kernel came under the kernel before. The nearest that computes the same is e6, at 1.0089. How much of e16's remaining 1.85% is the one wait is open.

## Why the prediction was wrong, point by point

- **GpSimd's conversions, 1.4 to 1.6 us: wrong, the term with the largest error.** They take 3.72, three of them 11.1 us instead of 4.2 to 4.8. I priced them by [rows 8] for their shape and overlooked that the second operation had changed from a multiplication to a minimum; both stand in the diff. I gave bounds to the clips and to `ctx_product` because they were new, and none to this. In the changed kernel the chain behind them makes the whole start late. Taking them back gives only 2.1 us of the median (e1), since the turns of w2 and the clock stand right behind; in the kernel before the minimum costs 6.75% (e3).
- **VectorE, from w2's scale to the last clip at 34.9: right** once the conversion is right (34.6 in e1). Clips alone took 0.41 to 0.45 for 0.35 forecast, and one, beside a conversion, 1.33. The upper end was summed wrongly: 0.9 more for each of six clips is 5.4 us, not 3, and five reads at 0.7 are 3.5, not 3. Neither decided anything.
- **Last turn of w2 at 39.5, bounds 38.4 to 41: wrong.** It lands at 41.9 (e6). The mis-sized part is the queue: the last turn was issued at 38.1 and not at 35.5, because the issues stand behind one another on SP (from 31.8, the longest takes 3.27), which I had not priced. Behind its issue it landed after 3.7, close to the 3.5 of [rows 10]; the two ahead of it took 5.4 and 6.6. In the changed kernel this error is hidden behind the first.
- **The chain floors to up factor, 41.9: right** (42.1 in e1). `hidden(0)` does wait for it in the changed kernel, e7 and e11. In e1, e4 and e6, with the multiplication, it waits for up product 0 instead, since w2's last turn is later than forecast.
- **The clock: half right.** I allowed for 1.2 GHz in gate product 1, not in up product 0 nor for its scatter; filler is worth 2.4 and 2.3 us (e6, e10).
- **Start +0.1: wrong, +5.6.** In the changed kernel the conversion's chain accounts for all of it: the up factor came 5.35 us late and the start 5.5 behind its forecast. Taken away step by step, 2.9 are the conversion (54.09 to 51.15, e1), 1.5 the clock and what scatters with it (to 49.69, e6), and for the last 1.1 down to 48.6 the late landing of the last turn (41.9 for 39.5) is the likely cause, since in e6 TensorE runs without a wait from there; no run had it land earlier.
- **Gate product 7, 1.0 us: right in cause and size** (0.91; it went when its quantization was moved, e4). That the size agrees is partly luck: the slopes were to wait for VectorE's statistics and waited for `ctx_product(3)`, which had itself waited 1.36 us for its context.
- **L15: `finish(13)` with 0.2 in hand, price up to 1: taken at 0, measured 1.16**, its upper end. Its cause is `store(10)` behind `turn_h(15)`; it went with that order (e4).
- **Waits in the stretch, 1.1 us forecast (g4 0.1, g7 1.0): wrong, 5.7 lost.** L0 (w3's last turn) lost 1.06 us, u4 (`hidden(3)`) 0.87, L3 (the turn of h) 0.83 and g9 (tile 9's turn) 0.66, from start to start. Of these the prediction had named only L3, as a point without slack, and priced it at nothing; L0 and g9 it had not worked out, and for u4 its own times leave 0.1 us (`hidden(3)` at 58.0, wanted at 58.1), which it passed over. Of its other points without slack u5 and L2 cost next to nothing. A point with 0.1 us in hand is not worth 0 when the times ahead of it are uncertain by a microsecond.
- **`ctx_product` 2.5: right, 2.37 and 2.36**, and e12 shows that they cost nothing where they stand. Rival 2 (161.5 for products of 4.4 us) gave a higher time for a reason that didn't happen.
- **`sum_scores` 1.4 each: 1.20 + 1.01 and 1.20 + 0.23.** It stands on the fullest engine, ahead of `hidden(3)`.
- **Strided PSUM reads at 0 of 0 to 0.7: right**, four at 0.672 us as in [rows 12].
- **Insertions -1.05, tail -0.3: right** (last product 2.58, the last half of `finish` 0.48; tail -0.5).

The range ended at 161.0 because every rival took the conversion's price as known. With 3.72 in the same layout the last clip comes at 39.8, everything behind it five us later, and the forecast would have been about 163 (158.05 plus 5, an estimate). The remaining 4 are the waits in the stretch: in spans, the forecast was missed by 9.95 us, of which 5.5 are the start and 4.6 those waits (5.7 for 1.1), less 0.2 in the tail.

## What to carry to other kernels

Price an instruction by its operations as well as by its shape: a `tensor_scalar` whose second operation has changed is a new instruction, and needs bounds like one. When the bounding engine is full, look in the table of windows for the second one that is nearly full beside it: here most moves that mended one wait brought another of the same size (e8, e9, e13 to e18), and only the two in e4 gained clearly. A late path can hide another: price what stands right behind it before expecting its whole time back. An idle stretch of GpSimd is no free place for a two-input product as long as VectorE has half-precision clips there.

## What the runs showed of the hardware

- GpSimd, 128x1024, float32 to half: scale and multiply 1.12 to 1.36 us (e1), scale and minimum 3.72 (after), scale and maximum 3.72 (e2), minimum with a strided result 3.99 (e3).
- Two half-precision clips of 128x1408 on VectorE: 0.95 us, beside one GpSimd product of 128x1024 3.21 and 3.59. VectorE's float32 reduce of 128x1026 beside such a product took its usual 1.20 (e4). A float32 instruction on 8 columns took 0.23 us, and 0.94 to 1.41 when it began within a GpSimd conversion or quantization of 1.44 (e7, e11, e16; 0.53 near its end, e14).
- Three DMA turns of 16, 16 and 12 blocks issued one behind the other held SP's queue 6.5 to 8.4 us (e5, e4); their products started 1.6 to 2.5 us apart (e6, e10, e18).
- After an idle time of 2.7 to 3.3 us TensorE ran its next product wholly or mostly at 1.2 GHz (4.12 to 4.88 us instead of 2.54; e4, e7, e11, e14, e16); with matmuls that nobody reads in that time it stayed at 2.4 GHz (e6).
- ScalarE's read of 128x512 float32 from PSUM took 0.672 us with its elements 128 apart (four, then the next four), and 0.673 in the kernel before, where they are neighbours.
